# Attention block in steps of eight elements instead of four, on one core

## Chip, cores and metric

One core of a Trainium2 chip. The metric is the device time of one execution in microseconds; engines are TensorE (PE, its weight loads PEld), VectorE (DVE), ScalarE (ACT), GpSimd (POOL) and SyncE (SP, which only issues DMAs here).

## What is computed

x is 128 batch elements of 128 tokens of 384 features; adj is a mask of 128x128 per element. Six heads of 64, all in float32:

```python
q, k, v = heads(x @ Wq + bq), heads(x @ Wk + bk), heads(x @ Wv + bv)
scores  = einsum('bhqd,bhkd->bhqk', q, k) / sqrt(64) + where(adj, 0, -9e15)[:, None]
ctx     = einsum('bhqk,bhkd->bhqd', softmax(scores), v)
out     = layernorm(x + merge(ctx) @ Wf + bf)      # no scale, no shift, eps 1e-5
```

## The kernel before

A group is four elements (512 tokens); there are 32 groups, and a step handles one. The loop (`run_steps`, `Fori`) has two steps in its body; the first two steps and the last ones are written out. Each engine has a function `step` whose order is its queue, and waits on semaphores by count (`past(engine, semaphore, n)` waits until item n is done). Nothing is planned by a program: the order is written by hand.

Precision: weights, x and contexts are split into a rounded part and a rest (`hi`, `lo`), and a product is three matmuls for each of three chunks of the contraction (`split_product`, L423): nine matmuls of 512 columns for q or k (`qk_product`, L478), nine of 384 for V (`v_product`, L518) and for the output (`out_product`, L471).

TensorE's order in a step of group g (L573): `scores` (24 head products, pairs on the two halves of 64 rows, 48 instructions), two of the next group's six q/k products as `qk_halves` (each matmul as two of 64 rows into two PSUM banks), `ctx_product` of group g-1 (pairs on the two halves of 64 columns), the other four q/k products, four `out_product` of group g-1, four `v_product` of group g+1. PSUM has eight banks: scores_ps is 0 to 5, work_ps 6 and 7.

VectorE (L729): `mask_and_max` (scores plus mask, negated, with the maximum: six tiles an element, L676), `sum_halves` (adds the two banks of a halved product), `invert_sums`, `turn_x` (32x32 transposes of x from x_blocks, which a DMA has loaded block by block), `turn_blocks` (the same of the probabilities), `split_ctx` and `split_x` (the lo parts), `add_residual` and `find_stats`. ScalarE (L897): `exps` (six exponentials an element), copies of q and k (`copy_half`, `copy_qk`), `round_ctx`, `round_x` (the hi parts), `copy_v`. GpSimd (L1042): `normalise_probs`, `make_mask_bias`, `add_bias` (x plus bias row, from x_in into x_bias, each with eight places), `normalise_y` (rstd by a power, then the scaling).

The probabilities are transposed by two DMAs through DRAM: `store_blocks` (L332, from p_turned, two places) and `load_blocks` (L339, four DMAs into pT). SyncE's order in a step (L358) mixes them with the loads of x_blocks for three groups on (two places), x_in and adj, and the stores of y (y_sb, four places). In the last group three elements are transposed by TensorE instead (`transpose_p`, L549). In the ending ScalarE normalises the last elements (`normalise_late`), GpSimd only finds their scale.

## Time and profile before

| | us |
|---|---|
| median of 3 runs | 1001.83 (1001.54 to 1002.15) |
| the profiled execution | 1002.12 |
| its span, first to last instruction | 1000.3 |
| busy: PE, PEld | 991.7, 900.2 |
| busy: DVE, ACT, POOL | 706.7, 589.5, 633.1 |
| share of the 16 DMA engines | 64.8% (main queue) |

A row of instructions has its start or its count, the engine, the line of the kernel, the operation, what it writes and reads, and, in brackets, how long its engine stood idle before it and what ended that. Times are us from the span's start unless marked ns. Of neighbouring matmuls the distance of the starts tells the pace; the durations overlap. The granted clock of TensorE is at full speed (2.4 GHz) throughout all stretches but the last, whose mean is 0.96 of it.

### The profile page before, as it was taken

What the parts mean: (1) busy time and instruction counts of PE and PEld (TensorE: products, weight loads), DVE (VectorE), ACT (ScalarE), POOL (GpSimd) and SP (SyncE); (2) the same over time, 40 slices, a digit from 0 to 9 for tenths busy, and PEclk for the clock granted to TensorE, in tenths of its full rate; (3) what the DMA queues carried; (4) which work ended last, traced back from release to release, by engine and by line L of the source; (5) the groups of instructions that cost most, each with busy time, mean ns of one, the idle gap of its engine ahead of it and who ended that gap; (6) DMA issues with size and microseconds to landing.
All of it is one profiled execution on the core that took longest, in us unless ns stands there. A gap on an engine that the chain in (4) does not pass through costs nothing.

```text
span 1000.3 us, 27877 instructions
## 1 busy us (share of the span) xinstructions
PE 991.7 (99%) x7690; PEld 900.2 (90%) x7690; DVE 706.7 (71%) x2760; ACT 589.5 (59%) x2130; POOL 633.1 (63%) x653
## 2 busy tenths in 40 slices
PE   9999999999999999999999999999999999999997
PEld 8788999889999889998899988999988999889997
DVE  5676766867668667677676686766777766867667
ACT  4766545675446665466654566554666545675556
POOL 2446657567566576575675765766656657567566
PEclk9999999999999999999999999999999999999999
DMA  8776676666776666766667666667666676665543
GB/s 186 175 196 167 172 210 189 178 163 171 199 193 186 168 170 175 218 172 182 161 176 204 188 178 169 173 183 207 181 173 168 171 215 181 176 171 160 160 151 104
DMA packets 344780, 178.08 MB, mean 178 GB/s; under 512 B 228784, under 2 KB 328752, under 8 KB 344752
## 3 DMA queue, kind: packets, MB, share of 16 engines
q1 hardware_dynamic: 343264, 176.77, 64.8%
q10 hardware_dynamic: 1488, 0.98, 0.3%
q8 instruction: 12, 0.20, 0.1%
q14 instruction: 16, 0.13, 0.0%
HBM read 103.35 MB, written 74.32 MB: 178 GB/s over the span
## 4 chain that ended last, share of the span: by engine, by line
PE 97%; ACT 1%; DVE 0%; DMA 0%; issue 0%; POOL 0%; SPq 0%; POOLq 0%; DVEq 0%
PE work_ps L427 16%; PE work_ps L429 15%; PE work_ps L428 15%; PE scores_ps L446 9%; PE scores_ps L466 9%; PE scores_ps L427 7%; PE scores_ps L429 7%; PE scores_ps L428 7%; PE work_ps L508 6%; PE scores_ps L508 6%; ACT probs L866 1%; DMA x_in<-in_x 0%; ACT qT L894 0%; PE scores_ps L545 0%; PE scores_ps L556 0%
## 5 line engine op out<-in xcount | busy, mean ns | idle before, releaser
L866 ACT ACTIVATE probs<-probs,neg_max 128x128 f32<-128x128 f32 x768 | 297.5, 392 | 87.9 <-DVE neg_max L676 87.9
L1038 POOL TENSOR_TENSOR probs<-probs,inv_sum 128x768 f32<-128x768 f32 x128 | 188.3, 1471 | 152.0 <-DVE inv_sum L699 152.0
L676 DVE CUSTOM_DVE_ANT_0 probs<-scores_ps,mask_bias 128x128 f32<-128x128 f32 x768 | 167.3, 286 | 127.9 <-PE scores_ps L446 127.2
L875 ACT COPY v_sb<-work_ps 128x384 f32<-128x384 f32 x128 | 61.3, 479 | 263.4 <-PE work_ps L429 263.4
L1033 POOL TENSOR_SCALAR y_sb<-y_sb,mean_var,rstd 128x384 f32<-128x384 f32 x120 | 198.4, 1653 | 21.5 <-POOL rstd L1023 21.5
L1023 POOL TENSOR_TENSOR rstd<-var_eps,minus_half 128x1 f32<-128x1 f32 x128 | 86.5, 676 | 168.5 <-DVE var_eps L720 168.5
L866 ACT ACTIVATION_READ_ACCUMULATOR probs<-probs,neg_max 128x1 f32 x768 | 146.9, 191 | 0.0
L1017 POOL TENSOR_TENSOR x_bias<-x_in,bias_row 128x384 f32<-128x384 f32 x128 | 128.9, 1008 | 7.7 <-DVE bias_row L829 7.7
L427 PE MATMUL scores_ps<-wf_hi,cT_hi 128*128 128x384 f32 x384 | 129.3, 337 | 0.0
L429 PE MATMUL scores_ps<-wf_hi,cT_lo 128*128 128x384 f32 x384 | 129.2, 336 | 0.0
L428 PE MATMUL scores_ps<-wf_lo,cT_hi 128*128 128x384 f32 x384 | 129.1, 336 | 0.0
L427 PE MATMUL work_ps<-wv_hi,xT_hi 128*128 128x384 f32 x381 | 128.0, 336 | 0.0
L429 PE MATMUL work_ps<-wv_hi,xT_lo 128*128 128x384 f32 x381 | 127.7, 335 | 0.0
L428 PE MATMUL work_ps<-wv_lo,xT_hi 128*128 128x384 f32 x381 | 127.4, 334 | 0.0
L692 DVE STREAM_TRANSPOSE p_turned<-probs 128x768 f32<-128x768 f32 x125 | 119.3, 954 | 1.1 <-DMA p_out<-p_turned 1.1
L446 PEld LDWEIGHTS scores_ps<-kT,qT 64*128 64x128 f32 x1536 | 88.2, 188 | 8.5 <-issue 7.7
L446 PE MATMUL scores_ps<-kT,qT 64*128 64x128 f32 x1536 | 94.4, 276 | 0.1
L466 PEld LDWEIGHTS scores_ps<-pT,v_sb 128*64 128x64 f32 x1536 | 83.2, 137 | 11.0 <-issue 10.7
L466 PE MATMUL scores_ps<-pT,v_sb 128*64 128x128 f32 x1536 | 90.9, 275 | 0.0
L651 DVE TENSOR_TENSOR cT_lo<-scores_ps,cT_hi 128x384 fp32r<-128x384 f32 x128 | 64.4, 542 | 28.9 <-ACT cT_hi L859 28.8
L707 DVE TENSOR_TENSOR y_sb<-scores_ps,x_bias 128x384 f32<-128x384 f32 x120 | 66.6, 555 | 21.0 <-PE scores_ps L429 21.0
L427 PE MATMUL work_ps<-xT_hi,wq_hi 128*128 128x512 f32 x198 | 80.7, 407 | 0.0
(94 smaller groups left out, 2068.1 us busy)
## 6 DMA issues: line engine op xcount, KB each, us to landing
p_out<-p_turned SPq DMA_DIRECT2D x125, 384.0 KB, 2.8
pT<-p_out SPq DMA_DIRECT2D x500, 96.0 KB, 2.8
x_in<-in_x SPq DMA_DIRECT2D x128, 192.0 KB, 2.9
x_blocks<-in_x SPq DMA_DIRECT2D x372, 64.0 KB, 2.3
out<-y_sb SPq DMA_DIRECT2D x120, 192.0 KB, 2.1
adj_u<-in_adj SPq DMA_DIRECT2D x32, 64.0 KB, 2.1
out<-xT SPq DMA_DIRECT2D x4, 192.0 KB, 2.7
out<-qT SPq DMA_DIRECT2D x4, 192.0 KB, 1.9
```

The lines of the kernel that those rows point to most:

```text
L427: nc.tensor.matmul(dst, s_hi, m_hi, start=k == 0, stop=False)
L428: nc.tensor.matmul(dst, s_hi, m_lo, start=False, stop=False)
L429: last = nc.tensor.matmul(dst, s_lo, m_hi, start=False, stop=k == n_chunks - 1)
L446: last = nc.tensor.matmul(scores_ps[:, score_cols(e, h)], qT[rows, c, h // 2, tokens(e)], kT[rows, c, h // 2, tokens(e)], start=True, stop ...
L466: last = nc.tensor.matmul(dst[half:half + HEAD, h // 2 * SEQ:(h // 2 + 1) * SEQ], v_sb[:, c % TURN * GROUP + e, h * HEAD:(h + 1) * HEAD], ...
L508: last = nc.tensor.matmul(half_bank(j, half), w[mat][rows, k, cols], moving[rows, c % TURN, k, :], start=k == 0 and w is w_hi and moving i ...
L676: last = nc.vector.tensor_tensor_reduce(out=probs[:, e, h, :], in0=scores_ps[:, score_cols(e, h)], in1=mask_bias[:, e, :], scale=-SCALE, s ...
L692: nc.vector.transpose(p_turned[:, e % 2, :, :, :].rearrange("p b h j -> p h b j"), probs[:, e, :, :].rearrange("p h (b k) -> p h b k", b=B ...
L866: last = nc.scalar.activation(probs[:, e, h, :], probs[:, e, h, :], ACT.Exp, bias=neg_max[:, e, h:h + 1], scale=-1.0, accum_out=row_sum[:, ...
L1017: nc.gpsimd.tensor_tensor(x_bias[:, slot, :], x_in[:, slot, :], bias_row[:, :], ALU.add).then_inc(x_biased, 1)
L1033: nc.gpsimd.tensor_scalar(y_slot(e, n), y_slot(e, n), mean_var[:, at, 0:1], rstd[:, at, 0:1], ALU.subtract, ALU.mult).then_inc(y_ready, 1)
L1038: nc.gpsimd.tensor_tensor(probs[:, e, :, :], probs[:, e, :, :], inv_sum[:, e, :].unsqueeze(2).broadcast_to([P, HEADS, SEQ]), ALU.mult).the ...
```

## The change

A step now handles a set of eight elements (two halves of four); there are 16 sets, the loop body is one step, and sets 0, 1 and from 14 on are written out. TensorE's order in step s is: scores of the first half, two halved products, scores of the second half, two halved products, the contexts of all eight elements of set s-1, eight whole q/k products, then by halves the outputs of set s-1 and the V of set s+1. Contexts are written by pairs of heads (m) over four elements, so `round_ctx` and `split_ctx` take 512 columns, three a half. V goes from PSUM to v_next, and `move_v` copies it to v_sb once the contexts of the set before are done. VectorE turns and splits x two elements at a time, and inverts four sums at once. x_in and x_blocks now hold one half (four elements), x_bias is gone (the bias is added in place), cT_hi and cT_lo hold one half. All banks have new places, with new waits. SyncE's order is new. In the ending all elements go through DRAM, there is no `transpose_p`, and 15 elements are normalised by ScalarE.

The core of the diff (helpers with four-element ranges turned into eight-element ones are left out; indentation is cut; in order SyncE, TensorE, VectorE, ScalarE, GpSimd):

```diff
+HALVED = 4
...
+SCORE_PAIRS = (((0, 3), (1, 4), (2, 5)), ((1, 4), (2, 5), (6, 7)))
+HALF_PAIRS = ((6, 7), (0, 3), (0, 3), (1, 4))
+CTX_BANKS = ((2, 5, 6), (7, 0, 3))
+WHOLE_BANKS = (1, 4)
+OUT_BANKS = (2, 5, 6, 1, 7, 0, 3, 4)
+V_BANKS = (2, 5, 6, 4, 1, 2, 5, 6)
...
+v_next = sb("v_next", [P, SET, HID])
...
+def load_x(s, e):
...
+    n = s * SET + e
...
+    past(sp, y_added, n - (SET if isinstance(n, int) and s >= LAST - 1 else GROUP))
+    sp.dma_start(x_slot(n, e), x[bass.ds(n, 1), :, :].rearrange("b p d -> p (b d)")
+                 ).then_inc(x_loaded[e % GROUP], DMA)
...
+def step(s):
+    more = not isinstance(s, int) or s + 2 <= LAST
+    if more:
+        load_x_blocks(s + 2, 0, range(KC * BLOCKS))
+    if is_step(s, LAST - 1):
         for e in range(GROUP):
+            load_x(s, e)
+    if not is_step(s, 0):
+        wait_for_reads(s - 1)
         for e in (0, 1):
+            store_blocks(s, e)
+        load_blocks(s, 0)
+        store_blocks(s, 2)
+        load_blocks(s, 1)
+        store_blocks(s, 3)
+        load_blocks(s, 2)
+    store_blocks(s, 4)
+    if more:
+        load_x_blocks(s + 2, 1, range(0, 6))
+    if not is_step(s, 0):
+        load_blocks(s, 3)
+    store_blocks(s, 5)
+    load_blocks(s, 4)
+    if more:
+        load_x_blocks(s + 2, 1, range(6, 12))
+    store_blocks(s, 6)
+    load_blocks(s, 5)
+    store_blocks(s, 7)
+    for e in (6, 7):
+        load_blocks(s, e)
+    if not is_step(s, 0):
+        for e in range(GROUP, SET):
+            load_x(s - 1, e)
+    if more:
+        for half in range(2):
+            load_adj(s + 2, half)
+    if is_step(s, 0):
+        return
+    for e in range(GROUP):
+        store_y(s - 1, e)
+    if not is_step(s, LAST - 1):
+        for e in range(GROUP):
+            load_x(s, e)
+        for e in range(GROUP, SET):
+            store_y(s - 1, e)
...
 def ending():
+    s = LAST
+    wait_for_reads(s - 1)
+    for e in (0, 1):
+        store_blocks(s, e)
+    for e in range(GROUP, SET):
+        load_x(s - 1, e)
+    for e in (2, 3, 4):
+        store_blocks(s, e)
+    for e in (0, 1):
+        load_blocks(s, e)
+    store_blocks(s, 5)
+    load_blocks(s, 2)
+    store_blocks(s, 6)
+    load_blocks(s, 3)
+    store_blocks(s, 7)
+    for e in range(GROUP, SET):
+        load_blocks(s, e)
     for e in range(GROUP):
+        load_x(s, e)
+    for e in range(GROUP, SET):
+        store_y(s - 2, e)
...
+def wait_for_score_pair(s, half, pair):
...
+        elif pair == 0:
+            past(pe, y_added, n - SET - 2)
+        elif pair == 1:
+            past(pe, y_added, n - SET - 1)
+            past(pe, v_copied, n + 4)
+        else:
+            past(pe, v_copied, n + 6)
...
+    elif pair < 2:
+        past(pe, max_found, n + 2 + pair)
+    elif is_step(s, LAST):
+        past(pe, y_added, n - 2 * SET + 5)
+    else:
...
+def ctx_group(s, half):
...
+        past(pe, v_moved, s * SET + SET - 1)
+    elif is_step(s, LAST):
+        past(pe, v_copied, BATCH - 1)
...
+            past(pe, v_copied, n + 3 + m)
+        elif half and m:
+            pe.wait_ge(qk_summed, sums(s + 2, 2))
+        elif not is_step(s, LAST):
+            past(pe, max_found, n + (6 if half == 0 and m < 2 else 7))
...
+def out_product(s, e):
...
+    pe.wait_ge(cT_split, ctx_count(s, half, KC - 1))
...
+    elif is_step(s, LAST - 1) and e in (3, 7):
+        past(pe, v_copied, LAST * SET + (6 if e == 3 else 7))
+    elif is_step(s, LAST):
+        past(pe, y_added, s * SET - SET + (3 if e < GROUP else 7))
+    elif e == 3:
+        pe.wait_ge(qk_copied, copies(s + 2, 2 * NJ - 2))
+    elif e == 7:
+        past(pe, v_copied, (s + 2) * SET + 3)
...
+def v_product(s, e):
...
+    elif is_step(s, LAST) and e >= GROUP:
+        if e < 6:
+            past(pe, y_added, (LAST - 2) * SET + e + 2)
+        else:
+            past(pe, max_found, LAST * SET + 5)
...
+def step(s):
+    if halved(s + 1):
+        scores(s, 0)
+        for j in (0, 1):
+            qk_halves(s + 1, j)
+    scores(s, 1)
+    if halved(s + 1):
+        for j in (2, 3):
+            qk_halves(s + 1, j)
+        for half in range(2):
+            ctx_group(s - 1, half)
+    for j in range(HALVED if halved(s + 1) else 0, 2 * NJ):
+        qk_product(s + 1, j)
+    for half in range(1 if is_step(s, LAST - 1) else 2):
+        if not is_step(s, 0):
+            for e in range(half * GROUP, (half + 1) * GROUP):
+                out_product(s - 1, e)
+        for e in range(half * GROUP, (half + 1) * GROUP):
+            v_product(s + 1, e)
...
+    scores(LAST, 0)
+    for e in range(GROUP, SET):
+        out_product(LAST - 2, e)
+    scores(LAST, 1)
+    for e in range(GROUP, SET):
+        v_product(LAST, e)
+    for s in (LAST - 1, LAST):
+        for half in range(2):
+            ctx_group(s, half)
+        for e in range(SET):
+            out_product(s, e)
...
+def turn_blocks(s, e):
+    past(dve, probs_ready, s * SET + e)
+    past(dve, p_stored[e % 2], s * GROUP + e // 2 - 1, per=DMA)
...
+def add_residual(s, e):
+    n = s * SET + e
     past(dve, out_done, n)
     past(dve, x_biased, n)
+    if not is_late(n):
+        past(dve, y_stored[e % GROUP], 2 * s + e // GROUP - 1, per=DMA)
+    nc.vector.tensor_tensor(y_slot(n, e), out_bank(s, e)[:, 0:HID], x_slot(n, e), ALU.add
+                            ).then_inc(y_added, 1)
...
+def step(s):
+    more = not isinstance(s, int) or s + 2 <= LAST
+    if not is_step(s, 0):
+        for e in range(GROUP):
+            mask_and_max(s, e)
+        for j in (0, 1):
+            sum_halves(s + 1, j)
+    for e in range(GROUP, SET):
+        mask_and_max(s, e)
+    if not is_step(s, 0):
+        for j in (2, 3):
+            sum_halves(s + 1, j)
+        invert_sums(s, 0, GROUP)
+    for e in (4, 6):
+        split_x(s + 1, e)
+    if not is_step(s, 0):
+        for e in (0, 1):
+            turn_blocks(s, e)
+    if more:
+        turn_x(s + 2, 0)
+    invert_sums(s, 4, 2)
+    if not is_step(s, 0):
+        for e in (2, 3):
+            turn_blocks(s, e)
+    if more:
+        turn_x(s + 2, 2)
+    turn_blocks(s, 4)
+    invert_sums(s, 6)
+    turn_blocks(s, 5)
+    invert_sums(s, 7)
+    if not is_step(s, 0):
+        for m in range(2):
+            split_ctx(s - 1, 0, m)
+    turn_blocks(s, 6)
+    if not is_step(s, 0):
+        split_ctx(s - 1, 0, 2)
+        add_residual(s - 1, 0)
+        find_stats(s - 1, 0)
+    turn_blocks(s, 7)
+    if not is_step(s, 0):
+        for e in (1, 2):
+            add_residual(s - 1, e)
+            find_stats(s - 1, e)
+        add_residual(s - 1, 3)
+        for m in range(KC):
+            split_ctx(s - 1, 1, m)
+        find_stats(s - 1, 3)
+    if more:
+        for e in (0, 2):
+            split_x(s + 2, e)
+        turn_x(s + 2, 4)
+        turn_x(s + 2, 6)
+    if not is_step(s, 0) and not is_step(s, LAST - 1):
+        for e in range(GROUP, SET):
+            add_residual(s - 1, e)
+            find_stats(s - 1, e)
...
+def ending():
+    s = LAST
     for e in range(3):
+        mask_and_max(s, e)
+    invert_sums(s, 0)
+    mask_and_max(s, 3)
+    for e in (4, 5):
+        add_residual(s - 2, e)
+    turn_blocks(s, 0)
+    invert_sums(s, 1)
+    add_residual(s - 2, 6)
+    turn_blocks(s, 1)
+    add_residual(s - 2, 7)
+    mask_and_max(s, 4)
+    invert_sums(s, 2)
+    for e in (5, 6):
+        mask_and_max(s, e)
+    invert_sums(s, 3)
+    mask_and_max(s, 7)
+    for e in (2, 3):
+        turn_blocks(s, e)
+    for e in (4, 5):
+        find_stats(s - 2, e)
+    invert_sums(s, 4)
+    for m in range(KC):
+        split_ctx(s - 1, 0, m)
+    invert_sums(s, 5)
+    turn_blocks(s, 4)
+    for e in (6, 7):
+        find_stats(s - 2, e)
+    turn_blocks(s, 5)
+    invert_sums(s, 6)
+    add_residual(s - 1, 0)
+    invert_sums(s, 7)
+    find_stats(s - 1, 0)
+    add_residual(s - 1, 1)
+    turn_blocks(s, 6)
+    find_stats(s - 1, 1)
+    for m in range(KC):
+        split_ctx(s - 1, 1, m)
+    add_residual(s - 1, 2)
+    turn_blocks(s, 7)
+    find_stats(s - 1, 2)
+    for e in range(3, SET):
...
+def round_ctx(s, half, m):
...
+    act.wait_ge(ctx_done, ctx_count(s, half, m))
+    if half and isinstance(s, int) and s >= LAST - 1:
+        past(act, v_done, BATCH - 1 if s == LAST else LAST * SET + GROUP - 1)
+    elif is_step(s, LAST):
+        past(act, out_done, s * SET - GROUP - 1)
+    else:
+        past(act, out_done, s * SET + half * GROUP - 1)
+    nc.scalar.copy(split_ctx_at(s, half)[0][:, m, :], ctx_bank(half, m)).then_inc(cT_hi_ready, 1)
...
+def move_v(s):
+    past(act, ctx_done, s * 2 * KC - 1)
+    past(act, v_copied, s * SET + SET - 1)
+    for e in range(0, SET, 2):
+        nc.scalar.copy(v_sb[:, e:e + 2, :], v_next[:, e:e + 2, :]).then_inc(v_moved, 2)
...
+        for e in (4, 6):
+            round_x(s + 1, e)
+        exps(s, 0)
+        copy_qk(s + 1, 0)
+        half_exps(s, 2)
+        copy_qk(s + 1, 1)
+        half_exps(s, 3)
+        exps(s, 2)
+        copy_qk(s + 1, 2)
+        half_exps(s, 6)
+        copy_qk(s + 1, 3)
+        half_exps(s, 7)
+        for e in (4, 5):
+            exps(s, e)
+        for q in range(12, 16):
+            half_exps(s, q)
+            copy_qk(s + 1, q - 8)
+        for m in range(KC):
+            copy_qk(s + 1, 8 + m)
+            round_ctx(s - 1, 0, m)
+        copy_qk(s + 1, 11)
+        move_v(s)
+        for m in range(KC):
+            round_ctx(s - 1, 1, m)
+    for e in range(GROUP):
+        copy_v(s + 1, e)
+    if more:
+        for e in (0, 2):
+            round_x(s + 2, e)
+    if not is_step(s, LAST - 1):
+        for e in range(GROUP, SET):
+            copy_v(s + 1, e)
...
+def step(s):
+    if not is_step(s, 0):
+        for e in range(GROUP):
+            add_bias(s - 1, e)
+        for e in range(SET):
+            make_mask_bias(s + 1, e)
+        for e in range(GROUP):
+            normalise_probs(s, e)
...
+    for e in range(GROUP, SET):
+        normalise_probs(s, e)
+    if is_step(s, 0):
+        return
     for e in (0, 1):
+        normalise_y(s - 1, e)
+    for e in (4, 5):
+        add_bias(s - 1, e)
+    normalise_y(s - 1, 2)
+    for e in (6, 7):
+        add_bias(s - 1, e)
+    for e in range(3, GROUP if is_step(s, LAST - 1) else SET):
+        normalise_y(s - 1, e)
...
 def ending():
+    s = LAST
     for e in range(GROUP):
+        add_bias(s - 1, e)
+    for e in range(3):
+        normalise_probs(s, e)
+    for e in (4, 5):
+        add_bias(s - 1, e)
+    normalise_probs(s, 3)
+    for e in (6, 7):
+        add_bias(s - 1, e)
+    for e in range(GROUP, SET):
+        normalise_probs(s, e)
+        normalise_y(s - 2, e)
+    for e in range(SET):
+        normalise_y(s - 1, e)
+    for e in range(SET):
+        add_bias(s, e)
+    for e in range(SET):
+        normalise_y(s, e)
```

## Rows read from the trace of the kernel before

**Rows 1.** Table of stretches, TensorE's busy us (instructions) first, of a step and the end.

```profile
511.00:541.68 30.68, 30.68 (x241) 27.91 (x240) 21.96 (x86) 18.07 (x66) 20.02 (x21) 1.00 0.67 182
...
966.50:1000.30 33.80, 28.31 (x262) 26.98 (x261) 23.27 (x98) 21.10 (x71) 20.54 (x28) 0.96 0.26 89
```

**Rows 2.** Chain that ended last: start us, us, what; scores of two steps.

```profile
511.07 2.88 PE scores_ps L446 x48
...
940.59 2.88 PE scores_ps L446 x48
```

**Rows 3.** TensorE in order of time (start us, us, engine, line): first scores.

```profile
27.25 2.95 PE L446 MATMUL scores_ps<-kT,qT 64*128 64x128 f32 x48
```

**Rows 4.** TensorE in order of time, around the changes of form in one step.

```profile
510.73 0.34 PE L429 MATMUL work_ps<-wv_hi,xT_lo 128*128 128x384 f32 x1
511.00 2.95 PE L446 MATMUL scores_ps<-kT,qT 64*128 64x128 f32 x48
513.70 0.48 PE L508 MATMUL work_ps<-xT_hi,wq_hi 64*128 64x512 f32 x2
514.02 0.39 PE L508 MATMUL work_ps<-xT_lo,wq_hi 64*128 64x512 f32 x2
...
517.67 0.40 PE L508 MATMUL scores_ps<-xT_hi,wk_lo 64*128 64x512 f32 x2
518.01 2.84 PE L466 MATMUL scores_ps<-pT,v_sb 128*64 128x128 f32 x48
520.78 0.50 PE L427 MATMUL work_ps<-xT_hi,wq_hi 128*128 128x512 f32 x1
521.11 0.40 PE L428 MATMUL work_ps<-xT_lo,wq_hi 128*128 128x512 f32 x1
```

**Rows 5.** ScalarE in order of time: copy of k, cast of two contexts.

```profile
527.23 0.69 ACT L894 ACTIVATE kT<-work_ps,bk_col 128x512 f32<-128x512 f32 x1 [0.51 <-PE work_ps L429]
527.81 0.85 ACT L859 CAST cT_hi<-scores_ps 128x384 fp32r<-128x384 f32 x2
```

**Rows 6.** VectorE in order of time: first and seventh masked tile, sum of halves.

```profile
512.94 0.29 DVE L676 CUSTOM_DVE_ANT_0 probs<-scores_ps,mask_bias 128x128 f32<-128x128 f32 x1 [4.11 <-PE scores_ps L446]
...
514.22 0.28 DVE L676 CUSTOM_DVE_ANT_0 probs<-scores_ps,mask_bias 128x128 f32<-128x128 f32 x1
...
518.27 0.69 DVE L687 TENSOR_TENSOR qT<-work_ps,qT 128x512 f32<-128x512 f32 x1
```

**Rows 7.** SyncE's queue in order of time: loads of x_blocks and pT, stores of probs.

```profile
523.29 2.11 SPq L322 DMA_DIRECT2D x_blocks<-in_x  x4
525.51 0.42 SPq L336 DMA_DIRECT2D p_out<-p_turned  x1
526.13 1.87 SPq L344 DMA_DIRECT2D pT<-p_out  x4
...
532.77 0.43 SPq L336 DMA_DIRECT2D p_out<-p_turned  x1
...
536.57 1.73 SPq L344 DMA_DIRECT2D pT<-p_out  x4
```

**Rows 8.** Page, part 6: DMA issues, KB each, median us to landing.

```profile
p_out<-p_turned SPq DMA_DIRECT2D x125, 384.0 KB, 2.8
...
out<-y_sb SPq DMA_DIRECT2D x120, 192.0 KB, 2.1
```

**Rows 9.** Page, part 5: busy us, mean ns of one, idle before.

```profile
L1038 POOL TENSOR_TENSOR probs<-probs,inv_sum 128x768 f32<-128x768 f32 x128 | 188.3, 1471 | 152.0 <-DVE inv_sum L699 152.0
...
L1017 POOL TENSOR_TENSOR x_bias<-x_in,bias_row 128x384 f32<-128x384 f32 x128 | 128.9, 1008 | 7.7 <-DVE bias_row L829 7.7
```

**Rows 10.** GpSimd in order of time: two rstd, a normalise_y between them.

```profile
537.99 0.56 POOL L1023 TENSOR_TENSOR rstd<-var_eps,minus_half 128x1 f32<-128x1 f32 x1
...
540.34 0.56 POOL L1023 TENSOR_TENSOR rstd<-var_eps,minus_half 128x1 f32<-128x1 f32 x1
```

**Rows 11.** TensorE in order of time: its last product.

```profile
994.47 0.34 PE L429 MATMUL scores_ps<-wf_hi,cT_lo 128*128 128x384 f32 x1
```

More of the change, by code:

```diff
@@ L73, in past, with run_steps, is_step @@
     eng.wait_ge(sem, value)
-def run_steps(eng, step, first=0, turns=TURNS):
-    for g in range(first, TURN):
-        step(g // TURN, g % TURN)
-    with eng.Fori(1, turns) as i:
-        for c in range(TURN):
-            step(i, c)
-    for g in range(turns * TURN, LAST):
-        step(g // TURN, g % TURN)
+def run_steps(eng, step):
+    for s in range(FIRST_LOOPED):
+        step(s)
+    with eng.Fori(FIRST_LOOPED, END_LOOPED) as i:
+        step(i)
+    for s in range(END_LOOPED, LAST):
+        step(s)
+def is_step(s, n):
+    return isinstance(s, int) and s == n
 def attention_block(nc, x, adj, wq, bq, wk, bk, wv, bv, wf, bf, out):
@@ new lines, in ctx_bank, with out_bank, v_bank @@
+        def ctx_bank(half, m):
+            return bank(CTX_BANKS[half][m])
+        def out_bank(s, e):
+            if is_step(s, LAST - 2) and e >= GROUP:
+                return bank(LAST_BUT_TWO_OUT_BANKS[e - GROUP])
+            return bank(OUT_BANKS[e])
+        def v_bank(s, e):
+            if is_step(s, 0) and e < GROUP:
+                return bank(6 + e % 2)
+            if is_step(s, LAST) and e >= GROUP:
+                return bank(LAST_V_BANKS[e - GROUP])
+            return bank(V_BANKS[e])
@@ new lines, in qk_bank, with is_late, stats_slot, y_slot @@
+        def qk_bank(s, j):
+            if is_step(s, 0):
+                return bank(6 + j % 2)
+            if is_step(s, 1) and j < HALVED:
+                return bank(HALF_PAIRS[1][j % 2])
+            return bank(WHOLE_BANKS[j % 2])
+        bias_bank = bank(5)[:, 0:HID]
+        def is_late(n):
+            return isinstance(n, int) and n >= LATE
+        def stats_slot(n, e):
+            return (GROUP + n - LATE) if is_late(n) else e % GROUP
+        def y_slot(n, e):
+            if is_late(n):
+                place = (xT[:, :, :, :].rearrange("p k n s -> p (k n s)"),
+                         kT[:, 1, :, :].rearrange("p m t -> p (m t)"),
+                         qT[:, 0, :, :].rearrange("p m t -> p (m t)"),
+                         kT[:, 0, :, :].rearrange("p m t -> p (m t)"))[(n - LATE) // GROUP]
+                return place[:, e % GROUP * HID:(e % GROUP + 1) * HID]
+            return y_sb[:, e % GROUP, :]
@@ new lines, in in_blocks, with x_slot, x_loads @@
+        def in_blocks(n):
+            return isinstance(n, int) and n // SET >= LAST - 1 and n % SET < GROUP
+        def x_slot(n, e):
+            if in_blocks(n):
+                blocks = x_blocks[:, :, :, :].rearrange("p k t j -> p (k t j)")
+                return blocks[:, e * HID:(e + 1) * HID]
+            return x_in[:, e % GROUP, :]
+        def x_loads(n, s, e):
+            if in_blocks(n) or not isinstance(n, int) or s < LAST - 1:
+                return 2 * s + e // GROUP
+            return 2 * (LAST - 1) + s - LAST + 1
@@ L391, in beginning @@
                 load_weight_rows(sp, "v", wv, 1)
-                for n in range(1, GROUP):
-                    load_x(n, n)
+                for e in range(1, GROUP):
+                    load_x(0, e)
                 load_weight_part(sp, "k", wk, 0)
@@ L444, in scores @@
+            def scores(s, half):
+                pe.wait_ge(qk_copied, copies(s, (half + 1) * NJ - 1))
+                if halved(s) and half == 0:
+                    pe.wait_ge(qk_summed, sums(s, HALVED - 1))
+                for e in range(half * GROUP, (half + 1) * GROUP):
                     for h in range(HEADS):
+                        t = e % GROUP * MATS + h // 2
+                        if t % 4 == 0 and h % 2 == 0:
+                            wait_for_score_pair(s, half, t // 4)
@@ L937, in ending @@
[L937 to L954 removed]
+                past(act, v_moved, n - SET)
@@ L1070, in ending @@
[L1070 to L1082 removed]
+                s = LAST
```

978 lines of the change are left out of this document (442 added, 536 removed).

## Prediction

> **What bounds the kernel now.** Read the table of stretches first: TensorE is busy for all 30.68 us of a step [rows 1]. Then the chain of waits, by the start of each step's scores: 14 steps from 511.07 to 940.59, so a step of four elements takes 30.68 us, and nearly every other step in the chain has that spacing to 0.01 us [rows 2]. No wait of another engine is long enough to show there; what the other engines do costs nothing as long as it comes in time. The start (scores of the first group at 27.25 [rows 3]) and the end, after the last scores at 966.5, are the only places where TensorE waits: in the last 33.80 us it is busy for 28.31 [rows 1]. So three sums decide: the length of a step in TensorE's own work, whether any other chain is longer than that, and the ending.
>
> **TensorE's own work.** The mix of products is the same (18 transposes of the ending go, some 1.7 us). What changes is how often the array's form changes. Normal pitches are 0.17 us for 384 columns and 0.23 for 512. Full to row form costs about 0.1 before the scores (510.73 to 511.00 is 0.27) and 0.1 in their first pair; scores to halves 0.09 (513.70 to 514.02), which their shorter last pair gives back; halves to contexts 0.11 (517.67 to 518.01) and some 0.05 in their first pair; contexts to whole products 0.1 at each side (520.78 to 521.11 is 0.33) [rows 4]. That is some 0.5 us for a round through the forms. Eight elements now take two rounds, 2 x 30.68 = 61.36; after the change one. The trace has no halves followed by scores. The nearest rows are scores to halves (nothing, net) and full to row form (0.2); I take nothing, since both keep 64 rows. The Trainium skill (TensorEngine Tiling (Array Packing), Key Properties) says that changing the tiling mode drains TensorE, and changing only the tile does not; by that rule the new order is free, by the dearer row it would take 0.2 more a step.
> A new wait lies in this sum: `out_product(s-1, 0)` needs all three `split_ctx` of its half, and ScalarE takes the third after `copy_qk(8+2)`, one product (2.04 us) ahead. From the rows: copy starts 0.2 after the product before, the cast 0.58 after that (527.23 to 527.81 [rows 5]), takes about 0.57 for 512 columns (0.47 for 384), VectorE's 512 wide operation 0.69 [rows 6]: 2.07 us, plus 0.1 to start again. It costs 0.1 us. Step without other waits: 61.36 - 0.5 + 0.05 = 60.9 us.
>
> **The ring that is new.** x_in has four places, not eight, and y_sb still four, and the order on SyncE is other. Follow one step from T, the start of its scores.
> VectorE masks an element in 1.28 us, first at T+1.94 [rows 6]. ScalarE's fourth exponentials end behind `copy_qk(3)` at T+15.7; VectorE inverts, splits x (four elements, 1.8) and turns element 0 by T+18.6. All this keeps TensorE fed: the second scores want the fourth maximum at T+7.8 (there at 7.1), the fourth halves the sixth at 11.7 (there at 11.4).
> SyncE issues four x_blocks loads in 2.2 us, four loads of pT in 1.95, a store and its step to the next in 0.6 [rows 7]. A store's data are there 2.8 us after its issue at the median [rows 8]; where four loads and a store run ahead of it, as for the fourth store, 3.8 (532.77, waited for until 536.57 [rows 7]). So: store 0 at 18.6, landed 21.4; loads of 0, store 2 at 23.4, loads of 1, store 3, loads of 2 from 26.6 (store 2 taken to land in 3.2, between the two rows) to 28.5; then without a gap store 4, six x_blocks, loads 3, store 5, loads 4, six x_blocks, store 6, loads 5, store 7 at 42.6. It lands at 46.4; loads 7 end at 48.4, and only then `load_x(s-1, 4)` is issued: x at T+51.3 (2.8 and a little, as a store [rows 8]).
> GpSimd stands in its order at `add_bias(s-1, 4)` since 44.6. Now it does two adds (1.0 each), `normalise_y(2)` (2.4), two adds, `normalise_y(3)` [rows 9, 10]: T+60.1. The store lands 2.2 later, at 62.3 [rows 8], and only then may VectorE put y of element 7 in the fourth place of y_sb: `add_residual(s-1, 7)` ends at T+62.9. The next step's scores may use bank 4, its second pair, when that is done. TensorE is there at 60.9 + 1.0 = 61.9. It waits 0.9 us in each step, and the ring sets the period: 61.8 us, 0.4 more than before. Queued behind the wait on TensorE are seven of eight tiles of scores, so masks and exponentials shift with it and the ring does not catch up.
> Bounds. Quick side: stores 2 and 7 land in 2.8, x in 2.1 as a store of y does [rows 8]: 2 us less, T+60.9, no wait, 60.9 us a step. Slow side: store 2 lands in 3.8 too, and VectorE, which still has 1.7 us of statistics to do after that add, starts its masks late by 0.6: 62.7 us.
> The Trainium skill (DMA: Bandwidth & Descriptors, Anatomy of one DMA) gives a DMA some 2.0 us and its bytes at 436 GB/s, which makes 2.9 us for a store of 384 KB. The median row agrees (2.8), the row behind four loads (3.8) does not. By the rule for all stores the ring would be 0.9 to 1.2 us shorter and would just not bind.
> Turns and splits of x in pairs, and sums of four at once, save VectorE starts of some 0.1 us; ScalarE's `move_v` adds four copies of 768 columns, about 3 us of its time at T+37 to 40, ahead of `round_ctx` of the second half, which needs the products `out(s-1, 3)` (T+42.4) anyhow. Both are covered by idle time; uncovered, the copies would cost 3 us a step.
>
> **The beginning.** Up to the first scores nothing moves (27.25 [rows 3]). Then 18 products of 2.04, 12 of 1.56 and two scores of 2.8 are 61.0 us, with changes of form and small waits 61.7: step 1 starts at 89.0.
>
> **The ending.** E is the start of the last set's scores; with 13 steps of 61.8 and one without its last eight products (60.9 - 12.5) it is at 89.0 + 803.4 + 48.4 = 940.8. TensorE's own work from there, with changes of form, is 54.6 us.
> GpSimd gets x of element 4 of the set before at E-0.5 (no x_blocks in that step), and has then two adds, y 2, two adds, y 3 (E+8.2), four adds of set 14 (E+12.1) ahead of its first `normalise_probs`: E+13.6. VectorE stands at `turn_blocks(15, 0)` until then, with `add_residual(13, 6)` behind it (E+15.3), then (13, 7) at 18.0 and the masks of elements 4 and 5 at 20.7. TensorE's last four V products each want one of these: they end at E+23.8 instead of 18.5, 5.3 lost.
> `split_ctx(14, 1, m)` stands behind `turn_blocks(15, 6)`; GpSimd comes to its probs after three normalise_probs (1.47 [rows 9]) and two normalise_y (2.4) from E+27.9: E+37.3, turned, statistics, three splits: E+41.4. TensorE wants them at 36.0: 5.4 lost. The last element's pT is stored at E+43 and loaded behind twelve others, there at E+54: 1.5 lost, 0.4 more in small waits. TensorE ends at E+67.3. Before, 5.7 us lie between its last start (994.47 [rows 11]) with 0.17 for that product and the span's end; with VectorE's 1.6 us for an element against 1.56 of TensorE over eight elements, 6.5: E+73.8.
> 940.8 + 73.8 = 1014.6 us of span. The profiled execution has 1.8 us outside its span (1002.12 against 1000.3) and lies 0.3 over the median: 1016.1, and I take 1016.
>
> **Rivals.**
> 1. The ring is too short to bind, the ending is as I say: 89.0 + 13 x 60.9 + 48.4 + 73.8 = 1002.9, as a run 1004. For it: only one of four stores shows 3.8. Against: SyncE's issues alone fill T+26 to T+46.
> 2. Faster: the ring doesn't bind and the ending's waits on VectorE and GpSimd are small, because x of set 13 comes before the last products and GpSimd has done its y by then. Then 89.0 + 791.7 + 48.4 + 61.1 = 990.2, as a run 992; with half of the 12.6 lost, 998. It decides at GpSimd's `add_bias(s-1, 4)`: if that starts before T+49, the whole queue behind it is 2 us early. For it: TensorE has no wait in 30 steps of before, and 0.5 us are saved in each of 14 steps; against it: x can't be asked for before `load_blocks(s, 7)`.
> 3. The slow side of the ring: 62.7 us a step, 1026 of span, 1028. For it: VectorE's statistics and masks are head to tail.
> 4. The change of form saves nothing, since halves to scores costs as much as it did to leave and enter: 61.4 a step and the ending, 1010.
>
> **How the numbers follow.** Forecast 0.39, rival 1 0.18, rival 2 0.25, rival 3 0.13, rival 4 0.05. Time: 1016. Range: from half of rival 2 down to 994, up to rival 3's 1027. Within 0.2% (999.8 to 1003.8, about what a measurement can tell) lie the low half of rival 1 and little else, 0.10; faster 0.25, slower 0.65.
>
> **What the profile will show.** Steps: the start of the first scores of each step, 60.9 apart if only forms count. The ring: `add_bias` of element 4 waiting for DMA into x_in for several us a step, `add_residual` waiting for the store of y, and TensorE's scores waiting for it. The ending: VectorE idle for GpSimd at `turn_blocks(15, 0)`, TensorE for VectorE at the V products and at `out_product(14, 4)`. A period of 60.9 with x_in landing before T+49 makes the ring wrong; a TensorE busy throughout its last 70 us makes the ending wrong. A period above 61.4 without that wait for y would mean another chain that I did not see.

## The result and the profile after

The changed kernel takes 1040.63 us (1039.52 to 1044.02, four runs) against 1001.82 us (1001.54 to 1002.15) beside it: 1.0393 times as long, 95% interval 1.0369 to 1.0417. The forecast was 1016, slower; the direction held, the size did not, and 1040.6 lies above the range that ended at 1027. The profiled execution's span is 1037.6 us, 23.0 more than the 1014.6 of the working and 37.3 more than before.

The table of stretches of after, cut where the first scores of a step start (start and end, length in us, then busy us of TensorE, its weight loads, VectorE, ScalarE, GpSimd, then the granted clock, share and rate of the DMA engines):

```profile
89.42:150.81 61.39, 61.30 (x481) 56.73 (x480) 42.03 (x152) 39.27 (x131) 27.13 (x28) 1.00 0.60 156
150.81:215.91 65.10, 62.74 (x481) 57.47 (x481) 44.97 (x159) 39.49 (x130) 41.25 (x42) 0.97 0.63 173
531.63:594.85 63.22, 61.69 (x482) 55.85 (x481) 44.34 (x158) 39.38 (x130) 40.48 (x41) 1.00 0.64 176
912.83:962.91 50.08, 48.89 (x410) 44.14 (x409) 34.64 (x140) 35.83 (x124) 32.29 (x33) 1.00 0.61 188
962.91:1037.60 74.69, 57.87 (x505) 55.27 (x504) 53.51 (x205) 37.41 (x128) 55.68 (x71) 0.93 0.57 185
```

Eight elements take 63.2 us where two steps of before took 2 x 30.68 [rows 1]. Thirteen steps lie between 89.42 and 912.83, 63.34 each in the mean. The one from 912.83, which has eight products less, is called the short step below, and what follows 962.91 the ending. The waits of TensorE over the whole run say for whom (engine, line waited for, us in total, times, longest):

```profile
PE scores_ps L587 <- DVE y_sb L900: 19.5, 13, 2.4
PE work_ps L540 <- DVE xT_lo L841: 4.3, 1, 4.3
PE scores_ps L540 <- DVE y_sb L900: 3.4, 2, 2.6
```

Once in every step but the first, scores wait for an add of the residual. This is the ring of the forecast: a chain of waits through SyncE, GpSimd, VectorE and TensorE that closes on itself and so sets the length of a step. The chain that ended last runs straight along it just ahead of the step at 594.85 (start us, us, what):

```profile
590.15 2.00 POOL x_in L1318 x2
592.15 0.53 POOL rstd L1324
...
592.84 1.66 POOL y_sb L1334
...
594.65 1.87 DMA out<-y_sb
...
596.64 0.57 DVE y_sb L900
```

Two adds of the bias, y 3, its store, and only then the add that puts element 7 in the fourth place of y_sb. It ends at 597.20, and TensorE goes on at 597.33 (in order of time, the idle us before and what ended them in brackets):

```profile
594.85 1.16 PE L587 MATMUL scores_ps<-kT,qT 64*128 64x128 f32 x16
...
597.33 1.50 PE L587 MATMUL scores_ps<-kT,qT 64*128 64x128 f32 x22 [1.32 <-DVE y_sb L900]
```

### The profile page after: what moved, and what is told of

Read it like the earlier page. It is cut to its first block, busy times and chain, and to the rows that moved or that the text cites. A ratio compares the mean times of both kernels' runs of the same rounds, so it can differ in the third digit from the quotient of the medians.

```text
span 1037.6 us, 27000 instructions
## 1 busy us (share of the span) xinstructions
PE 997.5 (96%) x7636; PEld 905.8 (87%) x7636; DVE 710.8 (69%) x2544; ACT 641.1 (62%) x2100; POOL 626.5 (60%) x653
## 3 DMA queue, kind: packets, MB, share of 16 engines
q1 hardware_dynamic: 345424, 179.13, 63.1%
## 4 chain that ended last, share of the span: by engine, by line
SPq 25%; PE 20%; DMA 16%; POOL 12%; issue 12%; DVE 8%; ACT 2%; DVEq 1%; POOLq 0%
SPq L408 15%; DMA p_out<-p_turned 9%; PE scores_ps L695 9%; SPq L384 7%; POOL x_in L1318 6%; DMA x_in<-in_x 4%; PE scores_ps L587 4%; POOL y_sb L1334 3%; DMA out<-y_sb 2%; SPq L400 2%; DVE xT_lo L856 2%; POOL rstd L1324 2%; DVE probs L869 2%; ACT probs L1127 2%; DVE p_turned L883 2%
## 5 line engine op out<-in xcount | busy, mean ns | idle before, releaser
L1318 POOL TENSOR_TENSOR x_in<-x_in,bias_row 128x384 f32<-128x384 f32 x120 | 118.5, 1014 | 104.1 <-DMA x_in<-in_x 104.1
L1142 ACT COPY v_next<-scores_ps 128x384 f32<-128x384 f32 x94 | 44.9, 480 | 144.7 <-PE scores_ps L542 143.6
L856 DVE TENSOR_TENSOR xT_lo<-xT,xT_hi 128x768 fp32r<-128x768 f32 x62 | 75.5, 1255 | 47.7 <-ACT xT_hi L1108 47.7
L587 PE MATMUL scores_ps<-kT,qT 64*128 64x128 f32 x1280 | 84.5, 282 | 19.7 <-DVE y_sb L900 19.5
L540 PE MATMUL scores_ps<-wv_hi,xT_hi 128*128 128x384 f32 x282 | 94.6, 335 | 4.2 <-DVE y_sb L900 3.4
L541 PE MATMUL scores_ps<-wv_lo,xT_hi 128*128 128x384 f32 x282 | 94.3, 335 | 0.0
L542 PE MATMUL scores_ps<-wv_hi,xT_lo 128*128 128x384 f32 x282 | 94.3, 335 | 0.0
L900 DVE TENSOR_TENSOR y_sb<-scores_ps,x_in 128x384 f32<-128x384 f32 x83 | 45.7, 551 | 57.5 <-PE scores_ps L542 28.2
L540 PE MATMUL scores_ps<-xT_hi,wk_hi 128*128 128x512 f32 x186 | 74.0, 398 | 0.0
L540 PE MATMUL scores_ps<-xT_hi,wq_hi 128*128 128x512 f32 x186 | 72.6, 390 | 0.4 <-ACT qT L1161 0.4
L541 PE MATMUL scores_ps<-xT_lo,wk_hi 128*128 128x512 f32 x186 | 72.6, 390 | 0.0
```

Of the source, the lines that this page charges most:

```text
L540: nc.tensor.matmul(dst, s_hi, m_hi, start=k == 0, stop=False)
L541: nc.tensor.matmul(dst, s_hi, m_lo, start=False, stop=False)
L542: last = nc.tensor.matmul(dst, s_lo, m_hi, start=False, stop=k == n_chunks - 1)
L587: last = nc.tensor.matmul(score_tile(e, h), qT[rows, half, h // 2, tokens(e)], kT[rows, half, h // 2, tokens(e)], start=True, stop=True)
L856: nc.vector.tensor_tensor(xT_lo[:, half, :, tok], xT_source(e, n, count), xT_hi[:, half, :, tok].bitcast(F32), ALU.subtract).then_inc(xT_s ...
L1318: nc.gpsimd.tensor_tensor(x_slot(n, e), x_slot(n, e), bias_row[:, :], ALU.add).then_inc(x_biased, 1)
```

## The experiments

All are edits of the changed kernel; the ratio is to the kernel before, with its 95% interval. "Period" is the mean of the thirteen steps and "ending" the time from the last set's first scores to the span's end, both from the profiled execution.

| kernel | us | ratio | period | ending |
|---|---|---|---|---|
| the change | 1040.63 | 1.0393 (1.0369 to 1.0417) | 63.34 | 74.7 |
| a1, x asked for earlier | 1010.81 | 1.0084 (1.0068 to 1.0101) | 61.54 | 71.9 |
| a2, x asked for later | 1067.34 | 1.0653 (1.0622 to 1.0683) | 65.26 | 76.2 |
| a3, splits of x first | 1036.35 | 1.0341 (1.0323 to 1.0360) | 63.07 | 76.1 |
| a4, probs first in the ending | 1038.02 | 1.0371 (1.0347 to 1.0396) | 63.00 | 74.5 |
| a5, y 2 and y 3 first | 1007.86 | 1.0058 (1.0041 to 1.0075) | 61.17 | 72.6 |
| a6, all four | 1009.26 | 1.0083 (1.0064 to 1.0102) | 61.16 | 73.4 |
| a7, a5 and a new ending | 1002.74 | 1.0007 (0.9998 to 1.0016) | 61.15 | 66.8 |
| a8, a7 with contexts first | 1003.28 | 1.0017 (1.0008 to 1.0026) | 61.23 | 66.9 |

**a1, x asked for earlier.** SyncE's order in a step:

```
-                for e in (6, 7):
-                    load_blocks(s, e)
                 if not is_step(s, 0):
                     for e in range(GROUP, SET):
                         load_x(s - 1, e)
+                for e in (6, 7):
+                    load_blocks(s, e)
```

> SyncE asks for x of elements 4 to 7 of the set before right behind store 7, ahead of the last two loads of pT, not behind them: some 5 us earlier in the step. Theory (the ring through x_in, GpSimd's normalise_y, the store of y and the add of element 7 sets the period of 63.3): x lands at T+47 instead of T+52.4, the wait of the second pair of scores goes, the period falls to what TensorE needs itself, 60.7 to 61.1, and the run to 1040.6 - 13 x 2.3 = 1010 to 1012; the two loads of pT that now come later by 2.2 us are not missed. Rival A (pT of the last elements is as late as x is): the gain is given back at the contexts, period 62.5 or more, run above 1030. Rival B (the period is lost to TensorE's forms or to contention, not to this ring): no change, 1040.

The run is 29.8 us shorter and the period 1.8; rivals A and B fall, though x came to GpSimd at T+49.5, not at T+47. The period stayed 0.4 above what was expected; the run time fits because the ending became 2.8 us shorter too, which was not expected. TensorE's waits for the add are 1.9 us in all instead of 19.5:

```profile
PE scores_ps L587 <- DVE y_sb L900: 1.9, 4, 0.8
```

Moving two loads behind four others, with no work taken away, brings back three quarters of the loss. The ring is shown as the cause; at 61.54 it still touches now and then.

**a2, x asked for later.**

```
                         load_adj(s + 2, half)
                 if is_step(s, 0):
                     return
+                for e in range(GROUP, SET):
+                    load_x(s - 1, e)
```

and the same lines taken away ahead of load_adj.

> The other direction: x of elements 4 to 7 is asked for behind the load of adj (one or two more issues of SyncE in front of it, 0.5 to 1.1 us). Theory of the ring: every microsecond of delay is a microsecond of period, 63.8 to 64.4 a step, run 1047 to 1055. Rival B (something else sets the period): within 2 us of 1040.6.

The sign is right, and 1.92 us a step is about twice what was expected: the two issues take 0.95 us in the changed kernel (585.50 below). What the expectation left out is TensorE's clock. The step at 613.31 of a2, first its wait and then three stretches of the table:

```profile
616.96 3.42 PE L586 MATMUL scores_ps<-kT,qT 64*128 64x128 f32 x32 [2.48 <-DVE y_sb L899]
```
```profile
613.31:617.00 3.69, 1.21 (x19) 1.02 (x18) 0.97 (x4) 2.04 (x3) 3.51 (x4) 0.92 0.40 126
617.00:620.10 3.10, 3.10 (x30) 3.10 (x32) 2.31 (x18) 0.16 (x1) 2.66 (x4) 0.54 0.81 255
620.10:624.30 4.20, 4.20 (x42) 3.57 (x40) 4.20 (x37) 3.99 (x19) 4.02 (x4) 1.00 0.21 76
```

After a wait of 2.48 us the granted clock is 0.54 for 3.1 us, the lower of its two levels; the 32 instructions take 3.42 us. In the changed kernel's step at 531.63 they follow a shorter wait and take 2.06:

```profile
534.19 2.06 PE L587 MATMUL scores_ps<-kT,qT 64*128 64x128 f32 x32 [1.40 <-DVE y_sb L900]
```

So 1.4 us are lost on top of the wait. In a2 the clock fell like this after eleven of thirteen waits of 2.0 us and more at this place; after those that ended at 682.23 (2.57 us) and 811.59 (2.24 us) it stayed at 1.00. These two steps take 64.34 and 64.00 us, about 1 more than the 63.2 of the change, which is what the two issues make; the eleven others take 65.0 to 67.1.

**a3, splits of x first** (VectorE's order in a step):

```
-                    invert_sums(s, 0, GROUP)
                 for e in (4, 6):
                     split_x(s + 1, e)
                 if not is_step(s, 0):
+                    invert_sums(s, 0, GROUP)
```

> VectorE's two splits of x for elements 4 to 7 stand ahead of its inversion of the sums, for which GpSimd's normalise_probs waits. In the changed kernel the two splits lie beside normalise_probs and take 3.1 us, elsewhere the same two take 1.8. Theory (VectorE's two operand work and GpSimd's work slow each other): the splits take 1.8 again, GpSimd's first six normalise_probs 1.47 to 1.5 instead of 1.66 each; but the first of them starts 1.8 us later than now if VectorE is not idle before the inversion. Net: the first turn ends 0 to 0.7 us earlier, and since the ring starts there, the period falls by as much: 62.6 to 63.3, run 1031 to 1041. Rival (the splits are slow for another reason, such as their place in memory): they keep 3.1 us, the first turn is 1.2 or more later, run 1050 or more.

In order of time, the changed kernel and then a3:

```profile
549.59 0.30 DVE L891 RECIPROCAL inv_sum<-row_sum 128x24 f32<-128x24 f32 x1 [0.51 <-ACT probs L1127]
549.81 3.09 DVE L856 TENSOR_TENSOR xT_lo<-xT,xT_hi 128x768 fp32r<-128x768 f32 x2
549.98 5.68 POOL L1339 TENSOR_TENSOR probs<-probs,inv_sum 128x768 f32<-128x768 f32 x3 [1.86 <-DVE inv_sum L891]
552.82 0.96 DVE L883 STREAM_TRANSPOSE p_turned<-probs 128x768 f32<-128x768 f32 x1
```
```profile
548.02 1.82 DVE L856 TENSOR_TENSOR xT_lo<-xT,xT_hi 128x768 fp32r<-128x768 f32 x2
549.75 0.30 DVE L891 RECIPROCAL inv_sum<-row_sum 128x24 f32<-128x24 f32 x1
551.74 0.98 DVE L883 STREAM_TRANSPOSE p_turned<-probs 128x768 f32<-128x768 f32 x1 [1.69 <-POOL probs L1339]
```
```profile
550.13 4.33 POOL L1339 TENSOR_TENSOR probs<-probs,inv_sum 128x768 f32<-128x768 f32 x3 [3.01 <-DVE inv_sum L891]
```

The same two splits take 1.82 us instead of 3.09, three normalise_probs 4.33 instead of 5.68: the rival (slow for another reason) falls. But VectorE now waits 1.69 us for GpSimd, so the first turn is only some 0.1 us earlier in the step (21.06 us after its start, not 21.19). The steps in the middle are as much shorter, 63.11 us against 63.22. The mean period is 0.27 shorter, which is less than what it differs by without a cause in the code: a4, whose steps are those of the change, has 63.00. The collision is real and its removal by order buys little, because the inversion pays for it.

**a4, probs first in the ending** (GpSimd): the three `normalise_probs(s, e)` stand ahead of the four `add_bias(s - 1, e)`.

> GpSimd does its first three normalise_probs of the last set ahead of the four adds of the bias to set 14, which no one wants soon. Theory (the V products of the last set wait for VectorE, which stands at turn_blocks(15, 0) until GpSimd is through its adds): turn 0 comes 4 us earlier, the V products end 3 to 4.5 us earlier, and if nothing behind takes over, the run is 1036 to 1038. Rival (the wait at out_product(14, 4) further on keeps the end where it is): no change, 1040.

The V products end 3.8 us earlier (19.5 us into the ending, not 23.3), and then the first and the fifth product of set 14 wait:

```profile
986.23 0.69 PE L540 MATMUL scores_ps<-wf_hi,cT_hi 128*128 128x384 f32 x1 [3.48 <-DVE cT_lo L841]
997.31 0.44 PE L540 MATMUL work_ps<-wf_hi,xT_hi 128*128 128x384 f32 x1 [3.13 <-DVE xT_lo L841]
```

The ending is 74.5 us, as good as unchanged: the rival is right. The run's 2.6 us lie within what its executions differ by (1034.2 to 1041.2); in the profiled one they are in the steps, which the edit does not touch.

**a5, y 2 and y 3 first** (GpSimd's order in a step; SyncE's as changed):

```
-                for e in (4, 5):
-                    add_bias(s - 1, e)
-                normalise_y(s - 1, 2)
-                for e in (6, 7):
+                for e in (2, 3):
+                    normalise_y(s - 1, e)
+                for e in range(GROUP, SET):
                     add_bias(s - 1, e)
```

with the range of y behind it starting at 4.

> Only GpSimd's order is changed, SyncE's stays that of the change: normalise_y(2) and normalise_y(3), whose statistics are there at T+47, stand ahead of add_bias(4..7) and no longer wait for x of element 4. Theory (what binds is not the late x itself, but that normalise_y(3), its store and so the fourth place of y_sb stand behind it): x may land at T+51 to T+52 as before, the adds of x end by T+56.5, the same time as VectorE wants them (T+56.7), the store of element 3 is issued by T+54; TensorE's wait in the second pair of scores goes, the period falls to 61.0 to 61.5, the run to 1008 to 1015. Rival (the late x itself binds): with its four adds ending at T+56.4 and more the adds of VectorE are still late by 1 us or more, period 62 or above, run above 1020.

32.8 us come back, more than in a1, with x as late as before:

```profile
505.40 1.65 POOL L1334 TENSOR_SCALAR y_sb<-y_sb,mean_var,rstd 128x384 f32<-128x384 f32 x1 [0.18 <-POOL rstd L1324]
509.35 3.95 POOL L1318 TENSOR_TENSOR x_in<-x_in,bias_row 128x384 f32<-128x384 f32 x4 [2.30 <-DMA x_in<-in_x]
```
```profile
457.42:518.49 61.07, 61.07 (x481) 56.14 (x480) 44.45 (x159) 39.39 (x130) 40.59 (x41) 1.00 0.67 182
```

GpSimd still waits for x until 509.35, T+51.9 of the step from 457.42, but y 3 is already normalised; TensorE is busy for all of the step. So the late x did no harm by itself: harm came from what stood behind it in GpSimd's queue. In the changed kernel GpSimd was idle just then:

```profile
585.83 2.01 POOL L1318 TENSOR_TENSOR x_in<-x_in,bias_row 128x384 f32<-128x384 f32 x2 [7.53 <-DMA x_in<-in_x]
```

**a6, all four together.**

> The four edits together: x asked for behind store 7, y 2 and y 3 ahead of the adds of x, VectorE's splits of x ahead of the inversion, and in the ending normalise_probs ahead of the adds. Theory: with the ring slack by 4 us and more every step takes TensorE's own 61.0 (13 x 61.0 from 89.3 to 882.3, +48.7: E at 931), the ending is 72 less the 3 to 4 us of the V products: span 999 to 1003, run 1001 to 1005, level with the kernel before. Rival (a further chain lies right behind this ring): steps keep 61.5 and more, run 1008 or above.

The rival's run time, though not for its reason: the steps are at 61.16, as in a5, so a1 and a3 add nothing once the ring is open. The ending is no better than in a5, since with a4's order the first product of set 14 waits 3.16 us for split_ctx.

**a7, a new ending.** GpSimd's part of it (VectorE's is rearranged in the same spirit):

```
+                for e in range(GROUP):
+                    normalise_probs(s, e)
+                    add_bias(s - 1, e)
+                for e in (4, 5):
+                    normalise_probs(s, e)
...
+                normalise_probs(s, 7)
+                for e in range(GROUP, SET):
+                    normalise_y(s - 2, e)
```

> On top of y 2 and y 3 ahead of the adds of x, the ending's order on VectorE and GpSimd is rewritten: GpSimd does normalise_probs of an element as soon as its sums are inverted, with one add of the bias behind each, and leaves normalise_y of set 13 for later; VectorE inverts a sum when its exponentials are there, turns elements 2 and 3 ahead of all statistics, and takes split_ctx(14, 0) and split_ctx(14, 1) before the turns that would make it wait. Theory (in the ending TensorE lost 1.3 us at the V products, 6.2 us in the products of set 14, and the span's end another 4.6 us because x of the last set was asked for behind all loads of pT, some of it at half clock): these 12 us come back but for 2 or 3, the ending is 62 to 64 us instead of 72.5, run 998 to 1000, slightly faster than the kernel before (1001.6). Rival (GpSimd and VectorE have more work than the ending gives them): 67 us or more, run 1003 or above.

The ending falls to 66.8 us, the run to 1002.74: level with the kernel before, 2.7 above the top of what was expected. Of the 12 us of which all but 2 or 3 were to come back, 5.8 came.

```profile
932.56:999.40 66.84, 55.64 (x505) 53.31 (x504) 53.48 (x205) 36.85 (x128) 52.66 (x68) 0.98 0.63 204
```

The kernel before, from the same scores on:

```profile
940.59:1000.30 59.71, 54.22 (x474) 50.14 (x474) 41.34 (x174) 36.21 (x130) 36.30 (x44) 0.98 0.38 124
```

Its ending holds 41.34 us of VectorE's work and 36.30 of GpSimd's, that of a7 53.48 and 52.66: x, y and probs of more elements are still open when the last set's scores start. That this work is what keeps the ending long is argued, not shown.

**a8, contexts of the last set first** on ScalarE and VectorE (`round_ctx(15, 0)` ahead of `normalise_late`, `split_ctx(15, 0)` ahead of the adds of elements 6 and 7 of set 14).

> On top of the rewritten ending: ScalarE and VectorE take the contexts of the last set's first half (round_ctx(15, 0), split_ctx(15, 0)) ahead of four rows of set 14 that nobody waits for. In the run before, TensorE waited 2.0 us there and 0.8 us at the second half. Theory (from 20 us into the ending VectorE works head to tail, 53.5 us of 66.8, so it sets the end whatever TensorE does): TensorE's last product ends 1.5 to 2 us earlier, the span's end moves by less than 0.5 us, run 1002 to 1003. Rival (TensorE's wait sets the end): the run is 1.5 to 2 us shorter, 1000.5 to 1001.3, and below the kernel before.

No gain, ending 66.9. But the step of the expectation that TensorE would be done earlier did not come true either: the wait at the split went from 1.76 to 0.2 us, and one in the contexts just ahead grew from 0.81 to 2.59 us:

```profile
977.37 0.44 PE L597 MATMUL work_ps<-pT,v_next 128*64 128x128 f32 x4 [2.59 <-issue]
```
```profile
976.72 0.55 DVE L900 TENSOR_TENSOR kT<-scores_ps,x_in 128x384 f32<-128x384 f32 x1
```

The profile names no releaser, but the kernel does: `ctx_group(15, 1)` waits for `add_residual(14, 6)`, and a8 has put just this add behind `split_ctx(15, 0)`. It ends at 977.27 and TensorE goes on 0.10 us later (in a7 at 974.67, and 0.09 later). The rows moved back as rows that nobody waits for were waited for. So a8 does not tell whether VectorE's work or TensorE's waits set the end of a7; that stays open. No version here beats the kernel before.

## Why the prediction was right and wrong

**The sum.** The 23.0 us by which the span was missed are 0.4 for the start of step 1 (89.42 for 89.0), 20.0 for thirteen periods (63.34 for 61.8), 1.7 for the short step (50.08 for 48.4) and 0.9 for the ending (74.7 for 73.8). The step of the forecast that failed is the size of the ring: "It waits 0.9 us in each step, and the ring sets the period: 61.8 us". The mechanism was right; the period measured 63.34, because the ring's own parts came to 63.14 and because a wait of TensorE could cost more than its length.

**TensorE's own work** was taken as 60.9 and is 61.07 in a step without waits on the ring (a5): 0.29 saved of 61.36, not 0.46. The missing 0.2 is the new wait at `out_product(s-1, 0)`, worked out as 0.1 and entered in the sum as 0.05: in a5 the first matmul of the outputs starts at 615.31, 0.32 us after the one before (0.23 without a wait), and the next 0.28 after it (0.17 without); the third `split_ctx` had ended at 615.26. Rival 4 (forms save nothing, 61.4) falls. Rival 1 (the ring doesn't bind) is just what a5 is: 1004 was said, 1007.9 measured. Of its span 3.5 us more than said lie in the thirteen steps (61.17 for 60.9) and 0.7 at the start; the ending is 1.2 shorter than said. Rival 2 put its point of decision at the right instruction (GpSimd's add of element 4) but the decision is what stands behind it: in a5 it starts at T+51.9, later than the T+49 named, and TensorE does not wait for it.

**The ring: mechanism right, length wrong.** SyncE's queue shows it (start us, us):

```profile
553.81 1.80 SPq L400 DMA_DIRECT2D p_out<-p_turned  x2
556.25 1.76 SPq L408 DMA_DIRECT2D pT<-p_out  x4
...
577.56 0.36 SPq L400 DMA_DIRECT2D p_out<-p_turned  x1
578.10 4.82 SPq L408 DMA_DIRECT2D pT<-p_out  x8
583.21 2.10 SPq L372 DMA_DIRECT2D x_in<-in_x  x4
585.50 0.95 SPq L390 DMA_DIRECT2D adj_u<-in_adj  x2
```

Cut into three parts, measured from the add that ends the ring once (533.50 + 0.56 = 534.06, row below) to its next end (597.20):

```profile
533.50 0.56 DVE L900 TENSOR_TENSOR y_sb<-scores_ps,x_in 128x384 f32<-128x384 f32 x1 [2.04 <-DMA out<-y_sb]
534.09 0.56 DVE L907 BATCH_NORM_STATS2 stats<-y_sb 128x6 f32<-128x384 f32 x1
...
535.78 0.29 DVE L869 CUSTOM_DVE_ANT_0 probs<-scores_ps,mask_bias 128x128 f32<-128x128 f32 x1 [0.62 <-PE scores_ps L587]
```

| part of the ring | predicted | measured |
|---|---|---|
| end of the add to the inversion | 14.6 (62.9 - 61.8 = 1.1, to 15.7) | 15.53 (to 549.59) |
| inversion to x asked for | 32.7 (15.7 to 48.4) | 33.62 (to 583.21) |
| x asked for to the end of the add | 14.5 (to 62.9) | 13.99 (to 597.20) |
| sum | 61.8 | 63.14 |

- First part, +0.9: the first mask comes 1.72 us after the add's end (535.78), not 0.84 (T+1.94 less 1.1). TensorE goes on 0.13 after the add, but the mask then stands behind VectorE's own statistics, which end at 535.15, and an idle time of 0.62. The row names TensorE for it; two others, of later steps, name nobody:

```profile
789.50 0.29 DVE L869 CUSTOM_DVE_ANT_0 probs<-scores_ps,mask_bias 128x128 f32<-128x128 f32 x1 [0.62 <-issue]
916.45 0.29 DVE L869 CUSTOM_DVE_ANT_0 probs<-scores_ps,mask_bias 128x128 f32<-128x128 f32 x1 [0.23 <-issue]
```

  The second is in the short step, outside the loop: there the mask starts 1.27 us after TensorE went on (915.18), not 1.59, so it is not the scores that take 1.59. In the looped steps the idle time is 0.62 whether TensorE's clock is at full speed (535.78) or not (789.50; 0.65 over the 3 us from 787.91). So about 0.5 of the 0.9 is the statistics, the delay that the forecast left to its slow side with 0.6; the other 0.4 is there only in looped steps, where VectorE goes round its loop between the two instructions, and that this is its cause is argued, not shown. From the mask to the inversion it is 13.8 us, as said.
- Second part, +0.9: the splits, taken at 1.8 us by their time beside an idle GpSimd, take 3.09, 1.3 more; 0.4 of it is given back by stores 2 to 7. No bound covered this, as the splits of before had never stood beside normalise_probs: none took over 0.56 us for 384 columns. The eight loads behind the last store take 4.82 us where 2 x 1.9 is their own; the rest is the wait for that store's data. From its issue to the asking for x it is 5.65 us, against the 5.8 of the forecast.
- Third part, -0.5: GpSimd has x 2.6 us after it was asked for, not 2.9; its two adds, y 2, two adds, y 3, the store of y and the last add are 0.2 shorter in all.

Of the thirteen steps the first has no such wait and takes 61.39, and two take 65.1 and 65.0. The one from 150.81 is in the table above; its wait of 2.35 us and what follows:

```profile
150.81:154.40 3.59, 1.23 (x18) 1.05 (x18) 1.60 (x5) 1.92 (x3) 3.41 (x4) 0.94 0.49 152
154.40:157.40 3.00, 3.00 (x28) 3.00 (x30) 2.24 (x18) 0.12 (x1) 2.65 (x4) 0.51 0.72 233
```

A longer wait, then half the clock, as in a2: the forecast had priced a wait at its own length. Why the wait is longer in these two steps stays open.

Two slips lie in the forecast's own sums. TensorE at T+61.9 and an add that ends at T+62.9 make a wait of 1.0 and a period of 61.9, not 0.9 and 61.8. And the slow side adds 0.6 for store 2 and 0.6 for the masks to that, which makes 63.1, not 62.7: close to the ring's 63.14, though of the two only the second came true. Even so the range would have ended near 1033. The 2.9 us for a store that the forecast sets beside its rows, from the Trainium skill (DMA: Bandwidth & Descriptors, Anatomy of one DMA), come from a fit for DMAs that GpSimd issues. The stores here are issued by SyncE, and their median is 2.8 us before and 2.9 in the changed kernel.

The largest fault of judgement lies beside the sum. Rival 3 (the slow ring, 62.7 us a step) had a chance of 0.13, and no case stood above it, so the range ended where the ring's known delays did, with nothing for one not in the rows.

**Halves to scores** costs nothing, as taken: the second scores start at once and take 2.59 us for 48.

**The ending** was right as a sum and near in its parts: V products, then `out_product(14, 4)`, which waited 4.3 us (the second of the waits shown first; said: 5.4). The remedy that seemed to follow from it, GpSimd's probs first, was not one (a4), because VectorE's own order made the next wait.

Which part of the change costs what: the ring 32.8 us, 2.1 of them in the ending (a5), the ending's order 5.1 more (a7), and the 0.9 left is within what a measurement tells from nothing. What the new order of TensorE saves, 14 times at most 0.29 us, and the forecast's estimate of 1.7 us for the transposes that are gone are used up by the ending: there TensorE stands idle for 11.2 us in a7 (66.84 less 55.64) and for 5.5 before (59.71 less 54.22). The lengths of the two endings themselves cannot be compared, as other products fall into them.

## What to carry to other kernels

- When places of a buffer are halved, follow each queue behind the wait that this makes: here no load was too late by itself, but an engine's order had put work that others waited for behind a wait that nobody needed yet. A change of order in GpSimd alone was worth 32.8 us.
- A sum around a ring takes everything that stands between two of its waits, with the durations that hold beside the neighbours it will have, and is made once more with the longer waits of TensorE priced above their length.
- Reordering one engine in an ending moves the wait to the next engine's order; write all queues' times side by side first.
